# An inverse transform whose matmuls read a copied, contiguous operand and move 128 columns instead of 64

## The reference

```python
def _stu_conv(phi, u, n):
    Vf = jnp.fft.rfft(phi, n=n, axis=0)
    Uf_p = jnp.fft.rfft(u, n=n, axis=1)
    Uf_m = jnp.fft.rfft(u * sgn3, n=n, axis=1)
    U_plus = jnp.fft.irfft(Vf[None, :, :, None] * Uf_p[:, :, None, :], n=n, axis=1)[:, :sl]
    U_minus = jnp.fft.irfft(Vf[None, :, :, None] * Uf_m[:, :, None, :], n=n, axis=1)[:, :sl]
    U_minus = U_minus * sgn[None, :, None, None]
    return (U_plus, U_minus)
...
out = jnp.einsum('btkd,k,kde->bte', U_plus, s, Mpp)
out = out + jnp.einsum('btkd,k,kde->bte', U_minus, s, Mpm)
```

## Time and profile before

| what | us |
|---|---|
| median of 3 runs | 3212.29 |
| lowest and highest run | 3210.49, 3217.34 |
| the profiled execution | 3219.43 |
| its span | 3217.6 |
| stage of the inverse transform, first matmul to end of last addition | 2254.2 to 2311.4 |

### The profile page before, as it was taken

How to read it: one execution, slowest core, us unless ns; L and a number is a source line. 1 busy time by engine, 2 the same in 40 slices (tenths; PEclk the granted TensorE clock), 3 DMA queues, 4 the chain that set the end, 5 groups by cost and what they waited for, 6 DMA issues and landing times. The chain is left out here.

```text
span 3217.6 us, 61524 instructions
## 1 busy us (share of the span) xinstructions
PE 2938.9 (91%) x23047; PEld 2310.9 (72%) x23047; DVE 1928.4 (60%) x3796; ACT 1414.4 (44%) x3058; POOL 1066.1 (33%) x1109
## 2 busy tenths in 40 slices
PE   5999998588887789999999999998979998999799
PEld 4777776333353559888888888887868887888555
DVE  5556574667744436666666666665257766775465
ACT  2555555111124315555555555554136665666200
POOL 3445452077714125555555555553000000000000
PEclk9999999799998799999999999999689999999799
DMA  7979772000003233344344343442100000000000
GB/s 176 192 171 192 170 168 59 13 1 1 1 3 115 108 82 83 80 88 87 81 87 87 83 87 82 88 87 54 52 7 1 1 1 1 1 1 1 8 23 30
DMA packets 419407, 213.43 MB, mean 66 GB/s; under 512 B 326260, under 2 KB 398604, under 8 KB 417324
## 3 DMA queue, kind: packets, MB, share of 16 engines
q1 hardware_dynamic: 401248, 199.32, 27.5%
q10 hardware_dynamic: 17868, 10.19, 1.4%
HBM read 177.82 MB, written 52.89 MB: 72 GB/s over the span
## 5 line engine op out<-in xcount | busy, mean ns | idle before, releaser
L1748 DVE TENSOR_TENSOR sl_vl_slot<-sl_psV_slot,sl_vh_slot 128x512 fp32r<-128x512 f32 x1024 | 636.1, 684 | 380.9 <-ACT sl_vh_slot L1730 380.8
L1730 ACT ACTIVATE sl_vh_slot<-sl_psV_slot 128x512 fp32r<-128x512 f32 x1024 | 529.5, 605 | 512.2 <-PE sl_psV_slot L1685 510.7
L1703 PE MATMUL sl_psY_slot<-sl_vl_slot,sp_Mh_sp 64*128 64x512 f32 x2048 | 418.2, 389 | 0.8 <-DVE sl_vl_slot L1748 0.3
L1703 PE MATMUL sl_psY_slot<-sl_vh_slot,sp_Mh_sp 64*128 64x512 f32 x2048 | 415.5, 386 | 0.0
L1703 PE MATMUL sl_psY_slot<-sl_vh_slot,sp_Ml_sp 64*128 64x512 f32 x2048 | 415.5, 386 | 0.0
L1661 POOL TENSOR_TENSOR sl_fl_slot<-sl_f_slot,sl_fh_slot 128x512 fp32r<-128x512 f32 x256 | 336.7, 1315 | 20.4
L1659 POOL CAST sl_fh_slot<-sl_f_slot 128x512 fp32r<-128x512 f32 x256 | 166.4, 650 | 451.5 <-PE sl_psV_slot L1685 450.5
L2106 DVE TENSOR_TENSOR ca_ptl_ca<-ca_psT_ca,ca_pth_ca 128x512 fp32r<-128x512 f32 (+1 forms) x272 | 183.8, 676 | 167.2 <-ACT ca_pth_ca L2043 167.2
L2043 ACT ACTIVATE ca_pth_ca<-ca_psT_ca 128x512 fp32r<-128x512 f32 (+1 forms) x272 | 158.9, 584 | 182.4 <-PE ca_psO_ca L87 178.7
L1703 PEld LDWEIGHTS sl_psY_slot<-sl_vl_slot,sp_Mh_sp 64*128 64x128 f32 x2048 | 208.8, 184 | 37.3 <-issue 12.7
L1703 PEld LDWEIGHTS sl_psY_slot<-sl_vh_slot,sp_Mh_sp 64*128 64x128 f32 x2048 | 208.4, 184 | 24.5
(11 more groups left out here) (398 smaller groups left out, 6230.1 us busy)
## 6 DMA issues: line engine op xcount, KB each, us to landing
sl_f_slot<-filt_hat SPq DMA_DIRECT2D x1024, 64.0 KB, 2.2
na_v_na<-na_windows SPq DMA_DIRECT2D x128, 390.0 KB
na_windows<-na_values SPq DMA_DIRECT2D x160, 113.8 KB, 6.5
na_values<-na_vo_na ACTq DMA_DIRECT2D x32, 260.0 KB, 7.0
u_hat<-fw_o_fwd SPq DMA_DIRECT2D x8, 1024.0 KB, 3.8
sl_u_slot<-u_hat SPq DMA_DIRECT2D x128, 64.0 KB, 2.2
y_hat<-sl_y_slot SPq DMA_DIRECT2D x128, 64.0 KB, 1.8
X<-in_x SPq DMA_DIRECT2D x8, 512.0 KB, 7.9
```

The costliest lines, as they stand in the source:

```text
L1703: mm = e.matmul(psY[half][:, :], left[pl][rows, :], right[pr][rows], start=kc == 0 and k == 0 and x == 0 and z == 0, stop=kc == KC - 1 and ...
L1730: e.activation(v_out(0, n, q), bank(4 * n + q), ACT.Copy).then_inc(S["v_high"], 1)
L1748: e.tensor_tensor(v_out(1, n, q), bank(m), v_out(0, n, q), ALU.subtract).then_inc(S["v_split"], 1)
```

## The change

ScalarE and GpSimd copy the operand of each group of eight r into a buffer `turned` with r outermost and channel innermost, so that the stationary operand of a matmul is contiguous. There are four such buffers of 128 x 1024 elements. GpSimd makes copies 1, 4, 6, 9, 12 and 14, ScalarE the other ten. The copies wait for the loads; TensorE waits for the copies and no longer for the loads. The matrix `kept` is made twice side by side, and each matmul moves 128 columns instead of 64: the second 64 columns of its result lie where the next matmul writes, and are overwritten by it. The last matmul of a group moves 64.

```diff
--- before.py
+++ after.py
@@ -1755,14 +1755,34 @@
 def spectral_outputs(nc, T, G):
 
     X = T["X"]
-    EARLY, RB, NP = 8, CH // NB, 4
+    EARLY, RB, NP, NT = 8, CH // NB, 4, 4
     GROUPS = R // RB
+    NG = B * GROUPS
+    by_pool = lambda n: n % 8 in (1, 4, 6)
+    of_act = [sum(not by_pool(m) for m in range(n + 1)) for n in range(NG)]
+    of_pool = [sum(by_pool(m) for m in range(n + 1)) for n in range(NG)]
     with ExitStack() as ctx:
         sb, pb = allocator(nc, ctx, "_inv")
         y_in = [G["y0"], sb("iv_y1", [128, C * R])]
-        inv, kept = sb("iv_m", [128, NB]), sb("iv_k", [128, NB])
+        turned = [sb(f"iv_t{i}", [128, RB, C]) for i in range(NT)]
+        inv, kept = sb("iv_m", [128, NB]), sb("iv_k", [128, 2, NB])
         ps = [pb(f"iv_ps{i}", [128, CH]) for i in range(4)]
-        S = Stage(nc, ctx, ["inv_loaded", "inv_kept", ("yh_loaded", B), "i_in_psum", "i_added"])
+        S = Stage(nc, ctx, ["inv_loaded", "inv_kept", ("yh_loaded", B), "t_act", "t_pool", "i_in_psum", "i_added"])
+
+        def turn(n):
+
+            b, g = divmod(n, GROUPS)
+            return turned[n % NT][:, :, :].rearrange("c r e -> c e r"), \
+                y_in[b][:, :].rearrange("c (e r) -> c e r", r=R)[:, :, g * RB:(g + 1) * RB]
+
+        def ready(e, n):
+
+            if n in (0, 1) or n // GROUPS == 1:
+                b = n // GROUPS
+                e.wait_ge(S["yh_loaded"][b], 16 * (NP if b else 1))
+            if n >= NT:
+                e.wait_ge(S["i_in_psum"], n - NT + 1)
+
         with S.block() as block:
             @block.sync
             def _(e):
@@ -1774,27 +1794,45 @@
                     q = C * R // NP
                     e.dma_start(y_in[1][:, p * q:(p + 1) * q], flat[:, p * q:(p + 1) * q]).then_inc(S["yh_loaded"][1], 16)
 
+            @block.scalar
+            def _(e):
+                for n in range(NG):
+                    if not by_pool(n):
+                        ready(e, n)
+                        dst, src = turn(n)
+                        e.activation(dst, src, ACT.Copy).then_inc(S["t_act"], 1)
+
+            @block.gpsimd
+            def _(e):
+                for n in range(NG):
+                    if by_pool(n):
+                        ready(e, n)
+                        dst, src = turn(n)
+                        e.tensor_copy(dst, src).then_inc(S["t_pool"], 1)
+
             @block.tensor
             def _(e):
-                e.wait_ge(S["inv_kept"], 1)
-                for b in range(B):
-                    e.wait_ge(S["yh_loaded"][b], 16 * (NP if b else 1))
-                    for g in range(GROUPS):
-                        n = b * GROUPS + g
-                        if n >= 4:
-                            e.wait_ge(S["i_added"], n - 3)
-                        for i in range(RB):
-                            r = g * RB + i
-                            mm = e.matmul(ps[n % 4][:, i * NB:(i + 1) * NB], y_in[b][:, r:r + (C - 1) * R + 1:R], kept[:, :],
-                                          start=True, stop=True)
-                        mm.then_inc(S["i_in_psum"], 1)
+                e.wait_ge(S["inv_kept"], 2)
+                for n in range(NG):
+                    if by_pool(n):
+                        e.wait_ge(S["t_pool"], of_pool[n])
+                    else:
+                        e.wait_ge(S["t_act"], of_act[n])
+                    if n >= 4:
+                        e.wait_ge(S["i_added"], n - 3)
+                    for i in range(RB):
+                        cols = 2 * NB if i + 1 < RB else NB
+                        mm = e.matmul(ps[n % 4][:, i * NB:i * NB + cols], turned[n % NT][:, i, :],
+                                      kept[:, :, :].rearrange("p z j -> p (z j)")[:, 0:cols], start=True, stop=True)
+                    mm.then_inc(S["i_in_psum"], 1)
 
             @block.vector
             def _(e):
                 e.wait_ge(S["inv_loaded"], 16)
-                e.tensor_tensor(kept[:, :].rearrange("p (c j) -> p c j", c=NCH), inv[:, :].rearrange("p (c j) -> p c j", c=NCH),
-                                G["keep"][:, :].unsqueeze(2).to_broadcast([128, NCH, NB // NCH]), ALU.mult).then_inc(S["inv_kept"], 1)
-                for n in range(B * GROUPS):
+                for z in range(2):
+                    e.tensor_tensor(kept[:, z, :].rearrange("p (c j) -> p c j", c=NCH), inv[:, :].rearrange("p (c j) -> p c j", c=NCH),
+                                    G["keep"][:, :].unsqueeze(2).to_broadcast([128, NCH, NB // NCH]), ALU.mult).then_inc(S["inv_kept"], 1)
+                for n in range(NG):
                     b, g = divmod(n, GROUPS)
                     e.wait_ge(S["i_in_psum"], n + 1)
                     x = X[:, b * L:(b + 1) * L].rearrange("e (j r) -> e r j", r=R)[:, g * RB:(g + 1) * RB, :]
```

## The result

The changed kernel takes 3187.27 us (median of four runs, 3184.98 to 3188.42); the kernel before took 3213.41 beside it. The ratio is 0.9915, with a 95% interval of 0.9901 to 0.9928. The forecast was 3187. The whole kernel is thus 0.85% faster, and the median says by itself little of where; the stage is read from the profile.

A forecast was written before the change was run, and what follows sets the result against it. TensorE's 256 matmul records bound the inverse transform, by low clock and strided weight load alike. Sum: 25.2 + 0.15 - 1.5 + 1.6 = 25.4 us off 3212.3, called 3187; range 3182 to 3200, forecast case 3183 to 3192.

The forecast's parts named there:

- The two halves are both needed: Inverse transform's matmuls: strided operand stays near 0.22 us a record at any clock, low clock at 0.213 with any operand.
- The clock rises: Inverse transform: with 128 columns moving, TensorE's clock rises 4.9 us after the stage's start, 2.8 to 6.8 allowed.
- From the first record to the last start: Inverse transform's 256 matmul records on TensorE: 30.4 us where it was 55.6, 25.2 us less.
- a sign of being wrong: Inverse transform: prediction wrong if 128-column records are spaced above 0.11 us at the high clock.
- 1.9 us was estimated for ScalarE: Operand copies of 1024 elements in the inverse transform: 1.05 us contiguous times strided factor 1.83, bounds 1.05 and 2 x 1.05.
- the wait for the first copy: Start of the inverse transform: TensorE starts at 2255.7 instead of 2254.22, 1.5 us lost (0.6 to 1.7).
- the step that called the second masked matrix hidden: Start of the inverse transform: VectorE's second masked copy, 64 columns, is hidden behind the first operand copy.
- The next stage: Stage after the inverse transform: its first 3.2 us of low-clock work takes half, 1.6 us less, if the clock stays up.
- the other end: Next stage's gain: 0 us kept as the lower end, should the clock not stay up over the 2 us gap.
- The copies as pace: Rival in the inverse transform: copies or a wavering clock take part of the gain, 3191 to 3203 us; chance 0.15.
- The clock that does not rise: Rival in the inverse transform: all records take 0.213 us, 3212.5 us, no change; chance 0.10.
- Slower through GpSimd: Rival in the inverse transform: GpSimd's six copies decide from 9.6 us a copy on; at 12 us, 3226; chance 0.03.

The follow-up runs named there:

- e1: Changed kernel with its contiguous copies, but every matmul moving 64 columns; 3224.06 us against 3219.51 for the kernel before, ratio 1.0011.
- e2: Changed kernel without the copies: strided operand, 128 columns a matmul; 3224.09 us against 3219.51 for the kernel before, ratio 1.0011.
- e5: Kernel before (strided operand, 64 columns) with 25 identity matmuls ahead of the stage to raise the clock; 3247.46 us against 3244.28, ratio 1.0009.
- e6: Changed kernel with 64 columns a matmul and 32 identity matmuls ahead to raise the clock; 3224.64 us against 3244.28 for the kernel before, ratio 0.9940.
- e7: Changed kernel with all 16 copies on ScalarE, none on GpSimd; 3217.97 us against 3244.28 for the kernel before, ratio 0.9916.
- e9: Changed kernel with 24 identity matmuls ahead, six behind, first copy in halves, GpSimd's first copy held back; 3217.51 us, ratio to the kernel before 0.9921.
- e3: Changed kernel with 32 identity matmuls ahead of TensorE's first wait in the stage; 3219.89 us against 3244.28 for the kernel before, ratio 0.9925.
- e4: Changed kernel with each of GpSimd's six copies made twice; 3193.05 us against 3219.51 for the kernel before, ratio 0.9917.
- e8: Changed kernel with 32 identity matmuls ahead of the stage and six behind its last group; 3216.23 us, ratio to the kernel before 0.9918.

## Why the prediction was right

**The two halves are both needed.** This was the core, argued from L2199, L350 and L1479, and e1, e2 and e5 show it: 0.213 us with the contiguous operand at the low clock, 0.218 to 0.220 with the strided one at either, 0.112 with both. e6 narrows the second half: what is needed is the high clock. Once it had been raised by other matmuls, 64 columns ran at 0.112 as well, so the doubled columns do nothing here but lift it. The estimate for the strided record at the high clock was 0.23; it is 0.22.

**The clock rises.** 4.9 us were taken from L1479, with 2.8 to 6.8 allowed. Measured: 4.3, 4.8 and 4.5 in the three profiles of the changed kernel, 3.2 in e2.

**TensorE.** From the first record to the last start 30.4 us were forecast; it is 30.5 (all 256 records take 30.80 us, the last of them 0.28). The doubled columns cost nothing: 0.111 to 0.112 us a record, as with 64 in e6. That is a hair above the 0.11 that the prediction had named as a sign of being wrong, a bound set without room for rounding; no cost of the doubled columns is behind it. No matmul waited for GpSimd.

**The copies.** 1.9 us was estimated for ScalarE from the factor 1.83 of the strided addition; it is 2.04 for most. GpSimd was bounded by 1.3, 2.4 and 3.8, and takes 2.01. The Trainium skill, "SBUF — State Buffer", section on Door 1, whose rule on 16-byte lines put the strided write on the dear side, agrees: 2.04 against 1.05 for the contiguous copy of the earlier trace rows. Whether the write, at a step of 128 elements, or the read, in runs of eight, is what costs was not tried.

**The start was mis-sized.** The sum has 1.5 us for the wait for the first copy. From the end of the slot stage to the first record it was 12.8 us, and is 2249.03 - 2234.19 = 14.8: 2.0 us. Two things were missed. The first copy took 2.4 us, not the 1.9 of the sum, and this 0.5 is the whole difference; it lies outside the 0.6 to 1.7 us that were allowed. And the step that called the second masked matrix hidden had the wrong price: the two took 2.25 us, from 2246.65 to 2248.90, and it is VectorE, not the copy, that the profile names as the releaser of the first record. VectorE's first one lasted until 2248.76, as GpSimd's copy, from 2246.50 to 2248.89, was ending. In e7, without that copy, the pair took 0.36 us; in e9, with GpSimd held back, 0.36 again. So the wait was for GpSimd. The Trainium skill, "SBUF — State Buffer", section on the two separate sides, has a rule for it: VectorE with two inputs in SBUF and GpSimd share a pair of ports that is locked for a whole instruction. The trace agrees, but for 0.13 us by which VectorE's record ends before GpSimd's. It happened to cost next to nothing here, because ScalarE's copy ended at 2248.88 as well; whether ScalarE's 0.4 us come from the same neighbour was not tried apart from e7, where the copy took 1.94.

**The next stage.** 1.6 us were counted with 0 as the other end. Its first stretch, start of L746 to first L754, went from 4.21 us to 2.65: 1.56. The other end was set too high. In e2 and e6 the clock fell in the same gap of 2 us and the stretch took 5.25 us, 1.04 more than before; in e3 it fell 0.4 us after the gap and the stretch took 4.35. So this term could have been -1.0. That it would be 1.6 rested on one row, the end of the slot stage, and it came out so in every profile of the changed kernel.

Sum of the measured terms: 55.5 - 30.5 = 25.0 from the records (first start to last start; the prediction's 55.6 is 55.5 in the trace), -2.0 at the start, +0.2 between the last record's start and L746, +1.55 in the next stage: with the roundings the 24.7 us of the stretch, where 25.4 was forecast. The medians say 26.1 us beside the first result, 23.6 and 25.5 in the repeats; the rest is scatter in parts the change does not touch. So that 3187.27 lies 0.3 us from the forecast is luck: the terms are good to 0.7 us together, and the medians scatter by more.

**The rivals.** The copies as pace: e4 and e7 show room on both engines. The clock that does not rise: seen in this stage with 64 columns (e1), never with 128. Slower through GpSimd: it takes 2.0 us a copy, far from the 9.6 that it would need.

What stays open is when the clock falls in the gap of 2 us between the stages. It stayed up in all three profiles of the changed kernel, in e4 and in e7, and fell in it in e2 and e6 and 0.4 us after it in e3; e8 and e9, with the gap cut to 0.73 us, kept it, but that is one profile each.

## What to carry to other kernels

Before costing a dense run of small matmuls, read the granted clock of its window. Here two bounds lay at the same height, the low clock at 0.213 us a record and the strided weight load at 0.218, and each hid the other, so that either repair alone bought nothing. Price a strided stationary operand at the high clock, not at the one that the trace happens to show. And try a small edit on both bounds together before discarding each by itself.

## What the runs showed of the hardware that was not expected

- A strided weight load of 128 fp32 columns holds a record at 0.22 us at clock 1.00 and at 0.50 (e2, e5); a contiguous one goes from 0.213 to 0.112.
- A stream of 64 fp32 columns with a contiguous operand did not lift a low clock in 54 us (e1), and held a high one for 28.7 us (e6). With the strided operand at 0.218 us a record it lost the high clock after 5.7 us (e5); 128 columns on that same operand kept it to the end of the stage (e2).
- A multiplication on VectorE of 64 columns with both inputs in SBUF took 2.1 us beside a copy on GpSimd, and 0.22 without it (e7, e9). The additions that read PSUM and X suffered little: 1.298 us beside the copies, 1.244 before, and 1.299 in e7, where only ScalarE copies, so that GpSimd is not the cause.
- ScalarE's copies of 2.04 us start 1.82 us apart (e7).
